# A two-layer hybrid network on one core: one prelude block for the grouped attention, moved norms in the feed-forwards, Hadamard low parts on VectorE

## What is computed

```python
x = x + _L0_attn_a_ref(_layernorm(x), ...)   # causal attention, 16 heads of 128, biases
x = x + _L0_ffn_ref(_layernorm(x), ...)      # SwiGLU 256 -> 1024, ternary weights, RMS norm inside
x = x + _L0_attn_b_ref(_layernorm(x), ...)   # delta rule over blocks of 16 tokens
x = x + _L0_ffn_ref(_layernorm(x), ...)
x = x + _L1_attn_a_ref(_layernorm(x), ...)   # grouped attention: 32 query heads of 8, 8 key heads, rotary
x = x + _L1_ffn_ref(_layernorm(x), ...)      # SwiGLU with Hadamard transforms and scales
x = x + _L1_attn_b_ref(_layernorm(x), ...)   # causal attention with linear position biases
x = x + _L1_ffn_ref(_layernorm(x), ...)
```

## Time and profile before

| | |
|---|---|
| median of 3 runs | 3950.96 us (3939.65 to 3962.98) |
| profiled execution, own time | 3935.7 us |
| its span, first to last instruction | 3933.8 us |
| TensorE busy | 3584.9 us, 91% |
| VectorE, ScalarE, GpSimd busy | 2498.3, 1941.6, 840.2 us |
| mean granted TensorE clock | 0.964 |

### The profile page before, as it was taken

The page is one execution under the profiler, slowest core; times in us unless marked ns, Lnnn a source line. Parts: engine busy times, 40 slices in busy tenths (PEclk is TensorE's granted clock), DMA queues, the critical chain, the costliest instruction groups (busy, mean ns, idle before and its releaser), DMA issues. The chain is left out here.

```text
span 3933.8 us, 54900 instructions
## 1 busy us (share of the span) xinstructions
PE 3584.9 (91%) x20008; PEld 2589.1 (66%) x20020; DVE 2498.3 (64%) x4874; ACT 1941.6 (49%) x4114; POOL 840.2 (21%) x826
## 2 busy tenths in 40 slices
PE   6999999999889997848999999789899999999989
PEld 5777877778666895623333333358777777777767
DVE  5666666656554665528888888344566666666643
ACT  3555555555442323304777777522455555555532
POOL 1111011100132452322000000020344443444410
PEclk9999999999889998867999999989999999999999
DMA  1000000000000000022111110010000000000000
GB/s 50 17 10 18 10 18 15 12 9 2 22 1 2 1 0 21 1 107 58 31 30 31 44 31 17 37 43 1 22 11 12 8 11 5 11 8 9 2 38 17
DMA packets 38792, 78.13 MB, mean 20 GB/s; under 512 B 7056, under 2 KB 17168, under 8 KB 35984
## 3 DMA queue, kind: packets, MB, share of 16 engines
q1 hardware_dynamic: 38544, 74.82, 6.4%
HBM read 56.97 MB, written 15.73 MB: 18 GB/s over the span
## 5 line engine op out<-in xcount | busy, mean ns | idle before, releaser
L1610 DVE TENSOR_REDUCE ga5m_nm<-ga5m_M 128x1 f32<-128x1024 f32 x512 | 604.4, 1218 | 85.6 <-PE ga5m_M L1514 82.4
L1599 ACT ACTIVATE ga5m_pr<-ga5m_E 128x512 f32<-128x512 f32 x1024 | 539.5, 603 | 209.8 <-PE ga5m_E L1550 206.3
L432 PE MATMUL at_A<-at_pT,at_V 128*128 128x512 f32 (+3 forms) x1536 | 519.8, 488 | 12.0 <-issue 5.0
L353 POOL TENSOR_TENSOR at_prob<-at_prob,at_slope_row 128x128 f32<-128x128 f32 (+7 forms) x256 | 369.7, 1447 | 577.4 <-DVE at_prob L650 577.3
L432 PEld LDWEIGHTS at_A<-at_pT,at_V 128*128 128x128 f32 x1536 | 283.9, 190 | 254.6 <-issue 204.3
L520 ACT ACTIVATE at_pT<-at_T 128x512 f32<-128x512 f32 (+3 forms) x768 | 347.1, 488 | 102.0 <-PE at_T L473 100.7
L1514 PE MATMUL ga5m_M<-ga5m_K,ga5m_Q 64*128 64x512 f32 x1024 | 304.0, 465 | 73.0 <-DMA ga5m_Q<-ga5m_zero 55.6
L1550 PEld LDWEIGHTS ga5m_E<-ga5m_Q,ga5m_K 64*128 64x128 f32 x1024 | 162.4, 185 | 313.1 <-ACT ga5m_pr L1599 304.8
L1550 PE MATMUL ga5m_E<-ga5m_Q,ga5m_K 64*128 64x512 f32 x1024 | 363.6, 447 | 3.9 <-ACT ga5m_pr L1599 3.6
L473 PE MATMUL at_T<-all_ident,at_prob 128*128 128x128 f32 x2304 | 336.4, 273 | 7.8 <-ACT at_pT L520 7.4
L473 PEld LDWEIGHTS at_T<-all_ident,at_prob 128*128 128x128 f32 x2304 | 268.3, 140 | 30.4 <-issue 7.7
(11 more groups left out here) (298 smaller groups left out, 8524.6 us busy)
## 6 DMA issues: line engine op xcount, KB each, us to landing
ga5m_Q<-ga_qs SPq DMA_DIRECT2D x64, 256.0 KB
at_raw_qk<-in_pqk SPq DMA_DIRECT2D x32, 256.0 KB, 2.9
ga_qs<-ga5s_part SPq DMA_DIRECT2D x8, 1024.0 KB
at_raw_v<-in_pv SPq DMA_DIRECT2D x16, 256.0 KB, 3.3
at_raw_o<-in_po SPq DMA_DIRECT2D x32, 128.0 KB, 2.0
ga5m_K<-ga_ks SPq DMA_DIRECT2D x32, 128.0 KB
all_X<-in_x SPq DMA_DIRECT2D x1, 2048.0 KB, 7.4
at_raw_t<-in_gu SPq DMA_DIRECT2D x8, 256.0 KB, 3.5
```

The lines of the kernel that those rows point to most:

```text
L353: nc.gpsimd.tensor_tensor(dst[:, 0:end], dst[:, 0:end], slope_row[n // 2 % 2][:, 0:end], ALU.add).then_inc(ramp_done, 1)
L432: mm = nc.tensor.matmul(bank[:, lo:GQ * P], V[b][:, kt, col:col + DH], pT[g][:, kt, lo:GQ * P], start=(kt == 0), stop=(kt == GQ * (g + 1) ...
L1599: nc.scalar.activation(pr[e % NR][:, :], Eb[e % 3][:, :], ACT.Exp, scale=scale).then_inc(e_done, 1)
L1610: nc.vector.tensor_reduce(nm[half % 2][:, m:m + 1], Mb[v % 2][:, :], AX.X, ALU.max, negate=True).then_inc(m_free[v % 2], 1)
```

## The change

In the grouped attention one block now holds the rotations, the values, the splitting, the stores, the fills and the first three loads. `part` is six buffers of 512 columns laid into the ternary weight tiles `w1` and `w2`, which nothing reads any more (`room`). TensorE's order is six rotations, eight value tiles, six rotations, eight value tiles. The key and query slots are filled whole, on GpSimd, between its first six adds. SP issues the loads of units 0 to 2 behind the stores of the ninth item. In the feed-forwards `turn` moves one step back, both `low_turned` stand at f = 6, and the next norm's steps are moved, its last group in two halves. In at1 the two comparisons of a piece move to the two steps behind. In the Hadamard stage the low parts of the first eight pieces are made on VectorE. The diff, cut to its core:

```diff
@@ causal_attention
-            ROUND = [(4 * (i // 2) + 2) * QT + (7, 9)[i % 2] for i in range(len(pieces))]
+            ROUND = [(4 * (i // 2) + 2) * QT + (8, 11)[i % 2] for i in range(len(pieces))]
+            CUT = {MEAN[i] + 2 + x: (i, x) for i in range(len(pieces)) for x in range(2)}
...
+            def cut(i, below):
+                v = index[("mean", MEAN[i] // QT, i)]
+                dve.wait_ge(a_free[v % 2], v // 2 + 1)
+                nc.vector.scalar_tensor_tensor((ups, dns)[below][i % 2][:, :], sc[i % 2][:, :],
...
@@ normed_swiglu, TensorE
-                    if f == 4 and g + 1 < NG:
+                    if f == 5 and g + 1 < NG:
                         turn(g + 1)
@@ GpSimd
-                if nxt is not None and f == 5 and g:
-                    next_root(g - 1)
+                if nxt is not None:
+                    if f == 1 and g >= 2:
+                        next_root(g - 2, range(GT))
+                    if f == 5 and g == NG - 1:
+                        next_root(g - 1, range(GT))
...
-                next_root(NG - 1)
+                next_root(NG - 1, range(2))
+                next_root(NG - 1, range(2, GT))
@@ VectorE
+                if f == 0 and nxt is not None and g >= 2:
+                    next_measure(g - 2, range(2, GT))
+                    next_shifted(g - 2, range(GT))
...
-                    if g:
+                    if g == NG - 1:
                         next_measure(g - 1, range(2, GT))
-                        next_shifted(g - 1)
-                if f in (6, 7) and g + 1 < NG:
-                    low_turned(g + 1, f - 6)
+                        next_shifted(g - 1, range(GT))
+                if f == 6:
+                    if g + 1 < NG:
+                        low_turned(g + 1, 0)
+                        low_turned(g + 1, 1)
+                    elif nxt is not None:
+                        next_normalise(g - 1, range(GT))
             low(NF - 1)
-            if nxt is not None:
-                next_normalise(NG - 2, range(GT))
...
                 next_measure(NG - 1, range(2))
+                next_shifted(NG - 1, range(2))
+                next_normalise(NG - 1, range(2))
             add(NG - 1, 1)
             if nxt is not None:
                 next_measure(NG - 1, range(2, GT))
-                next_shifted(NG - 1)
-                next_normalise(NG - 1, range(GT))
+                next_shifted(NG - 1, range(2, GT))
+                next_normalise(NG - 1, range(2, GT))
@@ hadamard_weights, VectorE
+            def low(k):
+                dve.wait_ge(high_done, k + 1)
+                nc.vector.tensor_tensor(place(w1[1], w2[1], k), full[k % 2][:, :],
+                                        place(w1[0], w2[0], k).bitcast(F32), ALU.subtract).then_inc(low_first, 1)
...
+                if 0 < k <= n1:
+                    low(k - 1)
@@ GpSimd
-            for k in range(n1 + n2):
+            for k in range(n1, n1 + n2):
@@ grouped_attention
+        NPART = 6
+        N = 512
+        spare = [t[:, :, :].rearrange("p c n -> p (c n)") for t in room]
+        part = [spare[i // 4][:, i % 4 * 2 * N:(i % 4 + 1) * 2 * N].rearrange("p (k n) -> p k n", n=N)
+                for i in range(NPART)]
...
+            order = ([("r", i) for i in range(2 * NJ)] + [("v", t) for t in range(NT // 2)]
+                     + [("r", i) for i in range(2 * NJ, 4 * NJ)] + [("v", t) for t in range(NT // 2, NT)])
+
+            @block.sync
+            def _(sp):
+                for i, (n, k) in enumerate(work):
...
+                    for x, done in enumerate((high_done, low_done)):
+                        sp.wait_ge(done, i + 1)
+                        for twice in range(2):
+                            dst = qs[k * 16:(k + 1) * 16, x, twice, :, cols] if k < 2 else ks[:, twice, x, :, cols]
+                            sp.dma_start(dst, part[i % NPART][0:M, x, :].bitcast(F32)
+                                         ).then_inc(stored[i % NPART], 16)
+                    if i == 3 * NJ - 1:
+                        sp.wait_ge(fill_done, 2 + 5 * NSLOT)
+                        for x in range(NPART):
+                            sp.wait_ge(stored[x], 64)
+                        for unit in range(NSLOT):
+                            load(sp, unit)
...
+                for what, i in order:
+                    if what == "r":
+                        multiply(i)
+                        if i:
+                            low(i - 1)
+                    else:
+                        copy_values(i)
+                        if i == NT // 2:
+                            low(len(work) - 1)
...
+                def fill_keys(slot):
+                    nc.gpsimd.memset(K[slot][:, :].bitcast(F32), 0.0).then_inc(kzero_done, 1)
+                    pool.wait_ge(kzero_done, slot + 2)
+                    for half in range(2):
+                        lo = half * HALF + NSTACK
+                        nc.gpsimd.memset(K[slot][lo:lo + 2, :].bitcast(F32), 1.0).then_inc(fill_done, 1)
+                    pool.wait_ge(fill_done, 2 + 5 * slot + 2)
+
+                def fill_queries(slot):
+                    for x in range(3):
+                        cols = slice(x * 1536, min((x + 1) * 1536, NQ * SEQ))
+                        nc.gpsimd.memset(Q[slot][:, cols].bitcast(F32), 0.0).then_inc(fill_done, 1)
+
+                fill_values()
+                for i, (n, k) in enumerate(work):
+                    M = jobs[k][2]
+                    pool.wait_ge(mul_done, 2 * (i + 1))
+                    if i >= 2:
+                        pool.wait_ge(low_done, i - 1)
+                    nc.gpsimd.tensor_tensor(rot[i % 2][0:M, :], ta[i % 2][0:M, :], tb[i % 2][0:M, :],
+                                            ALU.add).then_inc(add_done, 1)
+                    if i < 2 * NSLOT:
+                        (fill_keys, fill_queries)[i % 2](i // 2)
...
-                sp.wait_ge(fixed_in, 1)
-                for n in range(NSLOT):
-                    sp.wait_ge(ready[n], 4)
-                    load(n)
+                for i in range(NPART):
+                    sp.wait_ge(stored[i], 128)
                 for h in range(NH):
                     maxima(h)
```

More of the change, by code:

```diff
@@ L1100, in hadamard_weights @@
         full = [s.sb(f"full{i}", [P, NCOL]) for i in range(2)]
-        high_done, low_done, half_done = s.sem("high"), s.sem("low"), s.sem("half")
+        high_done, half_done = s.sem("high"), s.sem("half")
+        low_first, low_second = s.sem("low_first"), s.sem("low_second")
         acc = [s.ps(f"acc{i}", [P, NCOL]) for i in range(2)]
@@ L1388, in grouped_attention @@
             NR = 8
-            Q = [s.sb(f"Q{i}", [P, NQ * SEQ], F32R) for i in range(NSLOT)]
-            K = [s.sb(f"K{i}", [P, SEQ], F32R) for i in range(NSLOT)]
             pr = [s.sb(f"pr{i}", [P, 512]) for i in range(NR)]
@@ L1399, in grouped_attention @@
             Ob = s.ps("O", [P, 512])
-            fixed_in = s.sem("fixed_in")
-            ready = [s.sem(f"ready{i}") for i in range(NSLOT)]
-            q_in = [s.sem(f"q_in{i}") for i in range(NSLOT)]
             m_full = s.sem("m_full")
```

250 lines of the change are left out of this document (142 added, 108 removed).

## The result

The changed kernel takes 3834.0 us (median of 4 runs, 3831.7 to 3837.6) against 3945.3 us for the kernel before (4 runs): ratio 0.972 [0.967, 0.976]. The forecast was 3858 us, range 3836 to 3884: the direction is right, the time 24 us too long, and the range misses it by 2 us. The two profiled executions took 3935.7 and 3837.6 us, 98.1 us apart; the terms of the prediction add up to 93.5.

What follows compares the result with a forecast made beforehand. It held that time could be gained only where TensorE (91% busy) stands still or runs at half clock. 3935.7 - 44 - 38 - 12 + 0.5 = 3842.2 us, plus 15.3 to the median: 3858, range 3836 to 3884.

Steps and rivals of the forecast that it cites:

- The step to the median: Whole kernel: the profiled execution lies 15.3 us under the median of runs shown, so 3842.2 becomes 3857.5.
- The feed-forwards: ff2, ff4, ff6, ff8: shorter boundary stalls and fewer half-clock runs gain 9 + 9 + 13 + 7 = 38 us.
- the moved norm's loss: ff2 and ff4: the last-but-one group's norm now delays the last product, 1.9 us lost in each.
- I count 2.9 for three: ff2 and ff4: half clock behind the boundary stalls, 2.9 us regained over three boundaries.
- Prelude: Grouped attention: first row score 75 us behind the first rotary matmul (B), not 119; 44 us gained (36 to 53).
- the back-pressured price: Prelude: with its queue full SP finishes issuing at B+75; without back-pressure B+66.
- Rivals C: Prelude stores: price goes by the packet; at 298 ns no prelude gain, 3901; at 500 ns 3967 us; chance 0.04.
- E: Prelude: four 256 KB stores in flight move no faster than one; prelude gains 15, 3887 us; chance 0.03.
- Cuts: First attention: ternary cuts split over steps remove 12 of 15.6 us of TensorE waits (6 to 15.6).
- Hadamard: Hadamard stage: low(7) stands before the second of the last four parts; +0.5 us (-1 to +1.5).
- Rival B: Prelude: SP holds the block's end longer; prelude gains 36 and cuts 6; 3872 us; chance 0.15.
- Rival D: No back-pressure in the prelude (53 us), all half-clock runs and all cuts gone; 3838 us; chance 0.03.

Runs made afterwards that it cites:

- prelude_only: The kernel before with only the new grouped attention, its prelude as one block: 3918.9 us, ratio 0.993.
- prelude_fill: The kernel before with the new prelude and row scores computed again in the attention's last eleven steps: 3903.7 us, ratio 0.989.
- ff_only: The kernel before with only the new order in the four feed-forwards: 3892.6 us, ratio 0.988.
- turn_only: The kernel before with only turn behind gate_up(5) and both low halves behind hf(6): 3894.3 us, ratio 0.987.
- act_stores: The changed kernel with the last twelve stores (items 9 to 11) issued from ScalarE's queue, not SP's: 3832.1 us, ratio 0.972.
- late_loads: The changed kernel with the feed-forward norm put back in ff2 and ff4 and units 1 and 2 loaded in the next block: 3811.5 us, ratio 0.968.
- cuts_only: The kernel before with only the two cuts of each ternary piece moved to steps of their own: 3920.9 us, ratio 0.995.
- after_again: The changed kernel, unchanged, run again with a second profile: 3835.7 us, ratio 0.974.
- old_hada: The changed kernel with the low parts of the Hadamard weights back on GpSimd: 3835.7 us, ratio 0.972.
- norm_back: The changed kernel with the last-but-one group's norm put back behind the last low half in ff2 and ff4: 3829.6 us, ratio 0.973.
- late_fill: Norm put back and units 1 and 2 loaded in the next block, plus row scores computed again where they run out: 3813.0 us, ratio 0.967.

## Why the prediction missed

Two steps carry the 23 us between 3858 and the 3835.3 of nine runs.

**The step to the median failed: 11 us.** "That execution lies 15.3 us under the median of the runs shown (3951.0)" was right as arithmetic; the profiled execution lies 4.4 us under the median of 70 runs. Three runs of a kernel whose time spreads over 39 us were taken for its level, and that difference was carried over to another kernel in full. The spread goes with TensorE's granted clock. Some of the places lie in stages that the sum never looked at, since they aren't changed: prelude_only has two groups of runs and prelude_fill, with the end of the attention filled, one; and dr3 varies by 15 us. Where the longest runs of the kernel before lose their time stays open.

**The feed-forwards were mis-sized in their clock: 12 us.** The terms said 38 (29 to 46), the profiles 50 (and the medians of ff_only 46). The stalls were right: 28 us forecast (29.7 measured), the moved norm's loss of 1.9 each to the tenth. "The granted clock is 0.50 for 4.6 us behind the 4.2 us stall, worth 2 us; I count 2.9 for three" was wrong. One stretch was looked at, and only behind a boundary; ff2 and ff4 as wholes ran at 0.89 and 0.90, which one row for each would have told, and the busy time shows 8.8 and 6.0 us of clock given back, not 2.9. With ff6 and ff8 it is 20.4 us where some 10 were counted. These are one pair of executions, and luck has a part: ff2 alone took 137 to 143 us in the five profiles with its old order. That the profile's sum came within 5 us of the profiled time (3842.2 beside 3837.6) was luck too: the changed kernel's execution lost 7.4 us at the end of the attention, which hid more than half of this surplus. The credit was also put wrongly: the turn alone brings what the whole order does (turn_only), where the working gave the moved statistics 2.2 us at each middle boundary. Beside turn_only, they shorten the waits for low halves in ff4 by 0.5 us each at most (2.2 to 1.7, 1.8 to 1.4).

The other terms, which nearly cancel:
- Prelude 44 (36 to 53), measured 40.8 and in the medians 41. The order of events held, and each step within 3 us except TensorE's own end (B+62 for B+56), which nothing waits for. Taking the back-pressured price was right, and act_stores and late_loads show why: SP's queue goes at the pace of the transfers. The prediction located the limit at SP's issue; it is what has to be moved before the block's end. Rivals C and E (packets or small stores dear) fell: the last 36 us moved 242 GB/s.
- Cuts 12 (6 to 15.6), measured 15.1 in the profiles and 18 in the medians. The profile of cuts_only is 17.2 us shorter: 14.8 up to ff2, and 2.6 in ff2 itself, whose code is the same.
- Hadamard +0.5, measured +1.0 between the first two profiles and nothing in the medians. The stage varies by as much from one execution to the next: 34.5 us in after_again, 33.8 with the parts back on GpSimd (old_hada), 34.0 to 34.9 in the others with the old code.
- Rival B, SP holding the block longer, came true by 3 us of its 8. Rival D's time (3838) is nearest to the measured one, but not its reason: the back-pressure it denied was there.
- Rival A's mechanism showed in one place only, the last product's 3.7 us; norm_back took it away.

By the medians, 41 + 46 + 18 = 105 us (3 under, 8 over and 6 over their terms), and those of the 70 and the 9 runs differ by 104.8; by the profiles, 41 + 50 + 15 - 1 = 105, less the 7.4 lost in the attention.

The best kernel of the study is late_loads or late_fill (3811.5 and 3813.0), 24 and 23 us under the changed one on the same chip; the second spread less in its five runs, which may be chance.

## What to carry to other kernels

Before converting a profile's sum to a median, ask how the kernel's own runs spread and where its clock is near falling; a stage's mean granted clock, one row, prices that better than the half-clock stretch behind one stall. Where an issue queue looks like the limit, look at the DMA engines' share beside it: here, at 0.98, moving transfers past the barrier helped (13 us) and another queue did not. A sub-edit undone in the new kernel and done alone in the old tells which one earns the gain; here one of three earned all that the medians show, and the other two cancelled. And put one row per stage side by side for every profile there is: a stage that is 4 us shorter in three profiles of three tells what a median of five runs can't.

## What was not expected of the hardware

- The granted clock fell to 0.50 where TensorE had not stood idle for long. In prelude_only, as the row scores ran out:

```profile
2445.00:2450.00 5.00, 5.00 (x34) 2.04 (x34) 3.96 (x6) 3.64 (x8) 0.00 (x0) 1.00 0.00 0
2450.00:2455.00 5.00, 3.59 (x23) 1.17 (x24) 4.07 (x5) 2.67 (x6) 0.00 (x0) 0.96 0.00 2
2455.00:2460.00 5.00, 4.74 (x20) 1.03 (x16) 0.00 (x0) 3.35 (x7) 0.00 (x0) 0.50 0.03 7
```

It cost 0, 1, 7 or 18 us there in executions of the same code (the grouped attention's column above). With added matmuls that nothing needs, the clock of that stretch was 1.00, 1.00 and 0.95 in three profiles; without them, over the last 50 us, it was 0.95 or more in ten profiles (six of them with the old prelude) and 0.80 or 0.50 in four.
- It also fell at the end of the delta rule, in two profiles of 17, where TensorE had hardly stood idle: in late_loads it was busy 15.00 of the 15 us from 1402 to 1417, at a clock of 1.00, and 14.17 of the next 15, and the clock was 0.50 from 1426.7 to 1454.0. That cost some 10 us.
- VectorE's low parts did not slow down beside GpSimd's fills, where one beside a GpSimd addition had taken 1.80 us. The prelude's first five in the changed kernel, by line:

```profile
L1479 DVE TENSOR_TENSOR tern_w<-ga5p_rot,tern_w x5: 675/684/693, 1627.5 to 1644.3; 128x512 fp32r<-128x512 f32 x4, 64x512 fp32r<-64x512 f32 x1
```

The Trainium skill (SBUF — State Buffer, Who interferes with whom) says that a VectorE instruction with two SBUF inputs contends with a GpSimd instruction that reads SBUF, not with one that only writes it. By that, the trace agrees.
- Of a low part and a GpSimd addition that overlap, the one that begins first went at full pace. In the earlier trace rows the addition began 0.03 us ahead and the low part took 1.80 us. In the prelude's last six items the low part began some 0.15 us ahead and took 0.67 or 0.68 us, and the addition 1.63 to 1.65 in place of 1.26:

```profile
1662.21 0.67 DVE L1479 TENSOR_TENSOR tern_w<-ga5p_rot,tern_w 128x512 fp32r<-128x512 f32 x1
...
1662.36 1.65 POOL L1537 TENSOR_TENSOR ga5p_rot<-ga5p_ta,ga5p_tb 64x512 f32<-64x512 f32 x1 [1.93 <-DVE ga5p_tb L1473]
```
- A second queue did not issue faster: with twelve stores on ScalarE's, SP's 24 load DMAs took 25.5 us in place of 15.7, at 249 GB/s in place of 242 over the last 36 us. The Trainium skill (DMA: Bandwidth & Descriptors, Issuing engines are not separate DMA queues) says that the issuing engines share the same DMA engines. By that, the trace agrees.
